# Audio tower on one core: the products inside blocks of eight, for 64 keys at once in place of 32

## The reference, cut to what matters

```python
h = dct(x)                                   # (16, 938, 128), f32
q, k = exp(rmsnorm(xq @ Wq.T)), exp(rmsnorm(xk @ Wk.T))
v, g = xv @ Wv.T, sigmoid(xg @ Wg.T)         # 4 heads of 32
lam = exp(-exp(time_decay))
# per head, over time t:
A_t = lam * A_(t-1) + k_t v_t^T;  z_t = lam * z_(t-1) + k_t
att_t = (q_t^T A_t) / (q_t . z_t)
x = x + (g * att) @ Wo.T;  x = x + gelu(layernorm(x) @ W1.T) @ W2.T
```

## Time and profile before

| | |
|---|---|
| median of 3 runs | 1092.09 us (1091.17 to 1095.3) |
| span of the profiled execution | 1090.0 us |
| PE busy | 1058.7 us, 97% |
| VectorE busy | 886.6 us, 81% |
| ScalarE busy | 702.5 us, 64% |
| mean granted clock of TensorE | 0.990 |

### The profile page before, as it was taken

How to read it: one execution, slowest core, us unless ns; L and a number is a source line. 1 busy time by engine, 2 the same in 40 slices (tenths; PEclk the granted TensorE clock), 3 DMA queues, 4 the chain that set the end, 5 groups by cost and what they waited for, 6 DMA issues and landing times.

```text
span 1090.0 us, 44778 instructions
## 1 busy us (share of the span) xinstructions
PE 1058.7 (97%) x18851; PEld 800.2 (73%) x18851; DVE 886.6 (81%) x2749; ACT 702.5 (64%) x1258; POOL 293.5 (27%) x177
## 2 busy tenths in 40 slices
PE   6789999999999999999999999999999999999987
PEld 6668677877767778687877867777786777868664
DVE  6889788888988879788887988878788887979642
ACT  3357676576666757576575767657676675758643
POOL 5322132331223222132332223232122322213120
PEclk9799999999999999999999999999999999999999
DMA  5532133122312322132232312313242232214110
GB/s 179 168 91 88 52 94 102 60 89 72 125 51 74 106 76 89 51 127 70 65 97 73 108 51 78 117 59 89 60 130 57 74 105 77 71 51 127 52 39 18
DMA packets 51510, 91.55 MB, mean 84 GB/s; under 512 B 9552, under 2 KB 26608, under 8 KB 51312
## 3 DMA queue, kind: packets, MB, share of 16 engines
q1 hardware_dynamic: 51312, 88.69, 26.7%
HBM read 19.50 MB, written 9.78 MB: 27 GB/s over the span
## 4 chain that ended last, share of the span: by engine, by line
PE 95%; DVE 2%; ACT 1%; issue 1%; POOL 0%; DMA 0%; SPq 0%; DVEq 0%; ACTq 0%; POOLq 0%
PE bank L999 13%; PE bank L1004 11%; PE bank L1148 11%; PE bank L1170 10%; PE bank L1141 10%; PE bank L1176 10%; PE bank L1103 7%; PE bank L1078 4%; PE bank L1081 3%; PE bank L1121 3%; PE bank L1164 3%; PE bank L1086 3%; PE bank L1125 3%; PE bank L1041 3%; PE bank L1030 2%; PE bank L1056 1%
## 5 line engine op out<-in xcount | busy, mean ns | idle before, releaser
L1170 PE MATMUL bank<-xa,f1w 128*128 128x512 f32 (+1 forms) x256 | 120.5, 575 | 0.9 <-issue 0.9
L1148 PE MATMUL bank<-w,hid 128*128 128x128 f32 x1024 | 119.7, 275 | 1.5 <-ACT hid L565 1.5
L1141 PE MATMUL bank<-c,w 128*128 128x512 f32 (+1 forms) x256 | 119.2, 570 | 0.9 <-ACT c L559 0.9
L1148 PEld LDWEIGHTS bank<-w,hid 128*128 128x128 f32 x1024 | 116.9, 192 | 2.9 <-ACT hid L565 2.9
L539 ACT ACTIVATE px<-bank 128x512 f32<-128x512 f32 (+1 forms) x128 | 72.8, 568 | 63.5 <-PE bank L1086 55.2
L419 POOL TENSOR_TENSOR rr<-vv,nhalf 128x4 f32<-128x4 f32 x32 | 32.4, 1012 | 294.9 <-DVE vv L823 294.9
L565 ACT ACTIVATE hid<-bank 128x512 f32<-128x512 f32 (+1 forms) x128 | 70.2, 565 | 63.7 <-PE bank L1141 61.9
L1176 PE MATMUL bank<-hid,f2w 128*128 128x512 f32 (+1 forms) x256 | 107.5, 563 | 0.0
L1103 PE MATMUL bank<-qx,ki 128*32 128x16 f32 x7680 | 102.2, 193 | 1.5 <-DVE ki L866 1.5
L1103 PEld LDWEIGHTS bank<-qx,ki 128*32 128x32 f32 x7680 | 92.7, 110 | 13.7 <-issue 13.7
L804 DVE COPY_PREDICATED px<-mask,bank 128x512 f32<-128x512 uint32 (+1 forms) x128 | 88.5, 691 | 13.5 <-ACT px L539 13.5
(11 more groups left out here) (142 smaller groups left out, 2447.9 us busy)
## 6 DMA issues: line engine op xcount, KB each, us to landing
qx<-qq SPq DMA_DIRECT2D x256, 96.0 KB, 2.2
hs<-hs SPq DMA_DIRECT2D x32, 532.0 KB, 3.9
v<-v_f SPq DMA_DIRECT2D x16, 512.0 KB, 6.0
gz<-gate_f SPq DMA_DIRECT2D x16, 512.0 KB, 3.0
xT<-in_xT SPq DMA_DIRECT2D x16, 468.5 KB, 3.2
f1w<-in_fc1T SPq DMA_DIRECT2D x16, 256.0 KB, 3.2
f2w<-g_dram SPq DMA_DIRECT2D x16, 256.0 KB, 3.3
out<-t_sum SPq DMA_DIRECT2D x16, 256.0 KB, 2.5
```

The lines of the kernel that those rows point to most:

```text
L1141: mm(dst[:, 0:width[g]], w1[:, P * j:P * j + P], c1[:, cols(g)], start=True, stop=True).then_inc(w1_ok, 1)
L1148: last = mm(dst[:, P * i:P * i + P], hid[:, j, P * m:P * m + P], w2[:, j, :], start=(j == 0), stop=(j == 3))
L1170: mm(dst[:, 0:width[g]], f1w[:, P * j:P * j + P], xa[:, cols(g)], start=True, stop=True).then_inc(f1_ok, 1)
```

## The change

`pairs_b` takes two windows at once: 64 keys are the weights, the output is one of two halves of the partitions, and the moving operand has the j-th query of each of the eight blocks in the 64 frames, 32 columns. Each product now also has the cells of keys of one window with queries of the other; they go to cells of `DIAG` that the mask never selects. A call on four windows has 16 matmuls in place of 32, the one on two windows 8 in place of 16. Nothing else differs.

```diff
+PAIR = 2 * WIN
...
                 for j in range(EIGHT):
-                    for w in range(n):
-                        t0 = P * (c % 2) + WIN * w
-                        last = mm(D[WIN * w:WIN * w + WIN, :, WIN * w + j:WIN * w + WIN:EIGHT], ki[:, j, k0 + WIN * w:k0 + WIN * w + WIN],
-                                  x[:, :, t0 + j:t0 + WIN:EIGHT], start=True, stop=True)
+                    for o in range(n // 2):
+                        r, s0, t0 = slice(PAIR * o, PAIR * o + PAIR), k0 + PAIR * o, P * (c % 2) + PAIR * o
+                        last = mm(D[r, :, PAIR * o + j:PAIR * o + PAIR:EIGHT], ki[:, j, s0:s0 + PAIR],
+                                  x[:, :, t0 + j:t0 + PAIR:EIGHT], start=True, stop=True)
                 last.then_inc(pb_ok, 1)
```

## The result

| | before | after |
|---|---|---|
| median | 1092.66 us (1091.17 to 1095.3) | 1153.97 us (1153.54 to 1155.25) |
| ratio, 95% interval | | 1.0569 (1.0549 to 1.0588) |
| span of the profiled execution | 1090.0 us | 1151.7 us |

The time before is the median of four runs here, one more than the forecast's 1092.09 rests on. The change costs 61.3 us, or 5.7%.

What follows compares the result with a forecast made beforehand. The prediction took TensorE to bound the kernel: 36.5 us for wider rounds and 18.6 for seams make 55, added to a median of 1092.1 us for 1147 us, range 1124 to 1168.

Steps and rivals of the forecast that it cites:

- seams aren't free: Against the rival that going between the two packed shapes costs no drain: 1130 us, chance 0.13.
- the halves don't take turns: Against the rival that the two halves of a call don't overlap, 1.83 us a full call: 1252 us, chance 0.09.
- a fixed time per record: Rival: each record takes a fixed time per tile whatever its columns, rounds of 33 ns: 1097 us, chance 0.07.
- halving the count: Rival: handing out records, 10 ns each, paces a full call, so half the records gain: 1072 us, chance 0.05.
- What bounds the kernel: Whole kernel: TensorE, busy 97% of the span; time added to it is time added to the kernel.
- Part 1, the rounds: Calls of `pairs_b`: 64-column loads make rounds of 59 ns in place of 33, +36.5 us.
- the line through two widths: Weight loads: 33 ns for 32 columns and 112 for 128 give 0.82 ns a column, 59 ns for 64.
- Part 2, the seams: Where a record follows one of another shape: 160 new seams at 0.11 us and longer last streams, +18.6 us.
- the ends of the calls: At 80 call ends against unpacked work, the last stream is 13 ns longer, 1.0 us.
- Part 3, the rest: Semaphores, DMAs, order, merges and clock: nothing charged; the 0.4 us later result fits the gap before the merge.

Runs made afterwards that it cites:

- e2_alt: The changed kernel with 64-key products for even j only and 32-key products for odd j: 1235.86 us, ratio 1.1318.
- e8_cols40_contig: The changed kernel with only 40 of each 64 keys loaded and 8 neighbouring queries of each head read, neighbouring cells written: 1110.48 us, ratio 1.0171.
- e6_contig: The changed kernel, each product reading 8 neighbouring queries of each head in place of every eighth and writing 8 neighbouring cells: 1150.36 us, ratio 1.0536.
- e4_cols40: The changed kernel with only 40 of the 64 keys of each half loaded as weights, still 32 moving columns: 1150.10 us, ratio 1.054.
- e5_moving32: The kernel before, with its tiles of 32 keys, but each product streaming the changed kernel's 32 moving columns: 1138.57 us, ratio 1.0431.
- e9_before_contig: The kernel before, each product reading 4 neighbouring queries of each head in place of every eighth one: 1091.48 us against 1092.88, ratio 0.9984.
- e10_stride4: e8_cols40_contig with the 8 elements of each head 4 apart in the stream: 1150.19 us, ratio 1.0538.
- e11_stride2: e8_cols40_contig with the 8 elements of each head 2 apart in the stream: 1109.83 us, ratio 1.0165.
- e7_in_contig: The changed kernel, reading 8 neighbouring queries of each head, but with output cells still 8 apart: 1148.26 us, ratio 1.0525.

## Why the prediction was right, and where its terms were off

Forecast 1147 us (1124 to 1168), measured 1153.97; forecast +55, measured +61.3. The mechanism was right for the bound and the seams. For the rounds it named the load, and in the changed kernel the stream was just above it: that this cost so little was luck, as part 1 says. The runs speak against each rival: seams aren't free (e2_alt), the halves don't take turns (a call takes 0.94 us, not 1.83), a round isn't a fixed time per record (38 ns with 40 columns against 58 with 64 in e8_cols40_contig and e6_contig), and halving the count bought nothing (e8_cols40_contig has half the records and calls as long as before).

- **What bounds the kernel.** Right. PE's share stayed at 97%, its waits stayed, nobody waited for the changed line in its view after either, and each us on PE came out in the time.
- **Part 1, the rounds: +36.5 forecast, +42.2 measured.** The step that was off is "each matmul 32 moving columns (27 ns, under its load)". It priced a column at 0.84 ns from L1170, whose columns are neighbours. Columns 8 apart make rounds of about 60 ns (e4_cols40, e5_moving32); that is an estimate of 1.7 ns a column and 6 ns beside. For the kernel before this is harmless: under a load of 33 it doesn't show in the time (e9_before_contig). In the changed kernel the stream's round of 60 to 61 ns comes out just above the load's 58, and takes over: 120.1 us of calls against 117.7 ((146.2 - 128x0.223)/128 = 0.92 us, e6_contig) with a fast stream. The difference is larger at equal clock, because four calls of e6_contig fell into stretches at the lower clock and only one of the changed kernel, where a call has 1.92 us busy in place of 1.18 (row below the list). At full clock a full call takes 0.935 us against 0.903, which makes 4 us in all. So the load's price from the line through two widths was right (at full clock e6_contig has 112x0.903 + 16x0.897 = 115.5 us of calls and the kernel before 112x0.616 + 16x0.509 = 77.1: +38.4, forecast +36.5), and the stream was 4 us that the sum didn't have. That it was no more is luck: the load it was hidden under happened to be as long. With tiles of 40 columns the same oversight is worth 40 us (e4_cols40 against e8_cols40_contig), and with the stream alone, without any wider load, a call takes 0.96 us (e5_moving32).
- **Part 2, the seams: +18.6 forecast, 19 measured in e8_cols40_contig, some 23 in the changed kernel**, 0.13 us each (e2_alt). Charging the unseen pair of shapes as the seen one was right. What was too small is the price of the ends of the calls. The next line starts 0.133 us after the last record in e8_cols40_contig, 0.15 with loads of 64 columns (e6_contig) and 0.17 with a stream at distance 8 (the changed kernel, and e5_moving32 and e4_cols40 too). At the 80 ends against lines with 128 columns it was 0.119 before, so 0.05 came where 0.013 was charged; at the 48 ends against packed lines 0.155 and 0.125 came where 0.11 was. From start to start the changed kernel has 96x0.108 + 16x0.114 in front of its calls and 32x0.155 + 16x0.125 + 80x0.051 behind them, 23 us. Parts 1 and 2 then come to 65 us, more than 61.3. PE's idle time is 2 us shorter than before, and the mean clock was 0.994 against 0.990: the time lost to the lower clock is 1090.0x0.010 = 10.9 us before and 1151.7x0.006 = 6.9 after, an estimate of 4 us given back. Both profiled executions are single ones, so the last 2 us can't be told.
- **Part 3, the rest: 0.** Right. The merge behind a call still had its gap: nobody waited for the changed line, and PE's idle time went from 31.3 to 29.3 us.
- **Together.** By the steps between kernels: seams 19.0 (before to e8_cols40_contig), wide load 39.9 (to e6_contig, 1150.36 - 1110.48), distance 8 some 3.6 (to the changed kernel); 62.5 against 61.3. The last step is smaller than what times of different jobs can tell; the traces have 4 us in the calls at full clock and 128x0.017 = 2.2 behind them.

A call of the changed kernel on PE's timeline, in the stretch of the lower clock:

```profile
50.52 1.92 PE L1104 MATMUL bank<-qx,ki 128*64 128x32 f32 x32
```

## What to carry to other kernels

Before widening a tile of the array, price its weight load by its columns (0.82 ns each for f32, and some 5 to 7 ns, from rounds of 33, 38, 58 and 112 ns with 32, 40, 64 and 128 columns), not by how many instructions go: here four narrow tiles loaded side by side, two wide ones did half the loads at 58 ns each in place of 33, and halving the records won nothing. Count every place where packed work of one width meets work of another: each costs 0.1 to 0.17 us of an otherwise full TensorE, also between two packed widths. And price a stream by a row with the same distance between its elements; f32 elements 4 or 8 apart made rounds of 60 ns for 32 columns where neighbours fit under 38, which is free only as long as the load beside it is longer. When two limits lie close together, as load and stream did here, a forecast that comes out right doesn't tell which one holds; take each away by itself.

## What the runs showed of the hardware that was not expected

- f32 moving columns 4 or 8 apart in SBUF take longer than columns 1 or 2 apart: rounds of 60 ns against 38 for 32 columns (e4_cols40 and e10_stride4 against e8_cols40_contig and e11_stride2), where the 38 are the load's. By the estimate of 1.7 against 0.84 ns a column it is twice. For output cells 8 apart no price shows (e7_in_contig).
- A load costs by the columns it has, not by its tile's width: 40 columns in a tile of 64 allow rounds of 38 ns, 64 columns 58.
- What the engine needs from the last packed record to the next shape depends on that record's load and stream: 0.133 us with 40 columns and neighbours (e8_cols40_contig), 0.15 with 64 columns and neighbours (e6_contig), 0.17 with elements 8 apart, whether the tile loads 32 (e5_moving32, before 128 columns), 40 (e4_cols40) or 64 (the changed kernel).
- A full call of 64 records on four tiles is a fifth slower than its loads explain (0.62 against 0.52 us), with neighbours or elements 8 apart in its stream of 16 columns. The extra time lies in its first sixteen records and in records 32 to 40; what causes it is open.
